# A recurrence and a mixture of experts on one core: the downs six units behind the ups, the gate products three, and a rebuilt head

## The reference, cut to what matters

```
xw = x @ Wx + b
h_t = tanh(xw_t + h_{t-1} @ Wh)                 # 32 steps, one after another
xn  = h * rsqrt(mean(h*h) + 1e-5) * norm_scale
vals, idx = top_k(xn @ wg + bg, 4); gates = softmax(vals)      # 4 of 16 experts
for each expert e:
    u = xn @ w1[e] + b1[e];  a = min(u[0::2], 7);  b = clip(u[1::2], -7, 7)
    y_e = (a * sigmoid(1.702 a) * (b + 1)) @ w2[e] + b2[e]
out = x + h + sum over e of gate_e * y_e
```

## Time and profile before

| | us |
|---|---|
| median of 3 runs | 108.16 (108.02 to 108.65) |
| profiled execution, its own time | 107.47 |
| its span, first to last instruction | 105.7 |
| TensorE busy | 98.3 (93%) |
| VectorE, GpSimd, ScalarE busy | 67.2, 64.7, 61.7 |
| chain that ended last, TensorE's share | 82% |

### The profile page before, as it was taken

The page is one execution under the profiler, slowest core; times in us unless marked ns, Lnnn a source line. Parts: engine busy times, 40 slices in busy tenths (PEclk is TensorE's granted clock), DMA queues, the critical chain, the costliest instruction groups (busy, mean ns, idle before and its releaser), DMA issues.

```text
span 105.7 us, 1704 instructions
## 1 busy us (share of the span) xinstructions
PE 98.3 (93%) x549; PEld 83.6 (79%) x549; DVE 67.2 (64%) x179; ACT 61.7 (58%) x143; POOL 64.7 (61%) x77
## 2 busy tenths in 40 slices
PE   7778899989999999999999979999999999999980
PEld 2557789978999999999999958888777777777660
DVE  0302357976827996589787997668566556666740
ACT  3354836999755586667736646666555666655400
POOL 6004447997890995639963799689544566544400
PEclk9999999999999999999999999999999999999999
DMA  2999920007930000895048911995100000000003
GB/s 66 224 378 338 374 92 0 0 9 254 398 147 3 0 6 6 212 372 212 5 141 228 366 67 20 274 364 207 34 6 0 3 0 0 0 0 0 0 0 99
DMA packets 5000, 12.97 MB, mean 123 GB/s; under 512 B 752, under 2 KB 1792, under 8 KB 4992
## 3 DMA queue, kind: packets, MB, share of 16 engines
q1 hardware_dynamic: 4672, 12.69, 35.5%
q10 hardware_dynamic: 320, 0.18, 0.6%
HBM read 12.28 MB, written 0.59 MB: 122 GB/s over the span
## 4 chain that ended last, share of the span: by engine, by line
PE 82%; ACT 7%; DMA 2%; DVE 2%; POOL 2%; issue 2%; POOLq 0%; DVEq 0%; ACTq 0%
PE psA L806 20%; PE psB L806 19%; PE psY L836 12%; PE psR L836 7%; PE psR L753 5%; PE psY L753 3%; PE psM L836 3%; PE psR L848 2%; DMA wx_x_sb<-in_wx_x 2%; PE psR L745 2%; PE psM L760 2%; ACT small_h L450 2%; ACT psA L494 2%; PE psM L767 1%; ACT psA L503 1%
## 5 line engine op out<-in xcount | busy, mean ns | idle before, releaser
L414 POOL TENSOR_TENSOR actg<-act,gate_cols 128x512 f32<-128x512 f32 x31 | 39.4, 1281 | 12.5 <-DVE act L713 10.7
L696 DVE TENSOR_SCALAR lin<-psB,one_b1b 128x256 f32<-128x256 f32 (+1 forms) x48 | 26.0, 568 | 18.8 <-PE psB L806 18.8
L494 ACT ACTIVATE psA<-psA,lim_b1a 128x256 f32<-128x256 f32 (+1 forms) x48 | 23.8, 513 | 23.2 <-PE psA L806 23.1
L713 DVE SCALAR_TENSOR_TENSOR act<-lin,psA 128x512 f32<-128x512 f32 x32 | 22.0, 686 | 1.8 <-ACT psA L503 0.6
L503 ACT ACTIVATE psA<-psA,limit_col 128x512 f32<-128x512 f32 x32 | 21.1, 659 | 0.8
L806 PE MATMUL psA<-xn_hi,w_hi 128*128 128x256 f32 (+1 forms) x48 | 18.9, 394 | 0.2
L836 PE MATMUL psY<-actg,w_sb 128*128 128x256 f32 x64 | 17.2, 391 | 0.8 <-POOL actg L414 0.8
L806 PE MATMUL psB<-xn_hi,w_hi 128*128 128x256 f32 (+1 forms) x48 | 16.0, 333 | 0.0
L806 PE MATMUL psB<-xn_lo,w_hi 128*128 128x256 f32 (+1 forms) x48 | 15.6, 324 | 0.0
L806 PE MATMUL psB<-xn_hi,w_lo 128*128 128x256 f32 (+1 forms) x48 | 15.5, 323 | 0.0
L806 PE MATMUL psA<-xn_hi,w_lo 128*128 128x256 f32 (+1 forms) x48 | 15.5, 323 | 0.0
(11 more groups left out here) (87 smaller groups left out, 133.7 us busy)
## 6 DMA issues: line engine op xcount, KB each, us to landing
gate_cols<-gate_rows SPq DMA_DIRECT2D x16, 512.0 KB, 5.7
w_sb<-in_w SPq DMA_DIRECT2D x4, 512.0 KB, 7.3
w_sb<-in_w SPq DMA_DIRECT2D x4, 256.0 KB, 8.3
wx_x_sb<-in_wx_x SPq DMA_DIRECT2D x1, 320.0 KB, 5.9
wx_x_sb<-in_wx_x SPq DMA_DIRECT2D x2, 128.0 KB, 2.7
out<-yT SPq DMA_DIRECT2D x2, 128.0 KB, 4.3
out<-yT SPq DMA_DIRECT2D x1, 192.0 KB, 1.9
small_h<-in_small ACTq DMA_DIRECT2D x1, 105.0 KB, 2.8
```

The source lines that it names most:

```text
L414: nc.gpsimd.tensor_tensor(by_pair(actg[:, u % SUM_DEPTH, w]), by_pair(act[:, u % ACT_DEPTH, w]), gate_block(u, w), ALU.mult).then_inc(actg ...
L494: last = nc.scalar.activation(psA[u % 2][:, o], psA[u % 2][:, o], ACT.Relu, scale=-1.0, bias=lim_b1a[:, e0 + k:e0 + k + 1])
L696: last = nc.vector.tensor_scalar(lin[:, v % 2, o], psB[v % 2][:, o], one_b1b[:, e0 + k:e0 + k + 1], LIMIT + 1.0, ALU.add, ALU.min)
L713: nc.vector.scalar_tensor_tensor(act[:, v % ACT_DEPTH, 0:w], lin[:, v % 2, 0:w], 1.0 - LIMIT, psA[v % 2][:, 0:w], ALU.max, ALU.mult).then_ ...
```

## The change

LAG goes from 4 to 6, POOL_LAG from 2 to 3, and the rings to 8 and 6 units. All w1_high copies that were in slots 0 to 2 move in front of slot 0. The x products get other places: psX holds that of tile 1, psY those of tiles 0, 3 and 4, psR those of 2, 5, 6 and 7. Tiles 1 and 2 are multiplied after steps 1 and 2, tile 3 after step 4, tile 4 after step 6, tile 5 after step 7, tile 6 behind the laying of rstd, and tile 7 alone in front of step 28 (slot 10). The sums of tile 1 go to psX with semaphores of their own (sum1_mm, mean_ready) and leave the turns of psM; the raw logits of tiles 0 and 1 are made together behind them. In slots below LAG the gates' transposes stand between the halves of the up, and their copies in front of the gelu. The scaling of the gates is one tensor_scalar per tile instead of one tensor_tensor per pair. GpSimd's powers stay in front of the gate product of their slot.

```diff
--- before.py
+++ after.py
@@ -42,15 +42,15 @@
     UNIT0 = [sum(E // r for r in EXPERTS[:c]) for c in range(NC + 1)]
     NU = UNIT0[NC]
     WARM, WARM_START = 512, 5
-    LAG = 4
-    POOL_LAG = 2
-    ACT_DEPTH, SUM_DEPTH = 6, 5
+    LAG = 6
+    POOL_LAG = 3
+    ACT_DEPTH, SUM_DEPTH = 8, 6
 
 
     GROUP0 = list(range(CHUNKS[0])) + list(range(CHUNKS[0], NT + 1, 2))
-    W1_AHEAD, W1_SHARED = 5, 3
-    XW_AT = [0, 0, 1, 1, 2, 1, 2, 3]
-    XW_LATE = 5
+    W1_SHARED = 3
+    XW_AT = [0, 3, 0, 1, 2, 1, 2, 3]
+    XW_LATE = 7
     NQ = NT // 2
     PW = 2 * P
 
@@ -160,12 +160,14 @@
         w1_half_ready = sem("w1_half_ready")
         w1_hi_ready = sem("w1_hi_ready")
         m_mm = sem("m_mm")
+        sum1_mm = sem("sum1_mm")
         raw_mm = sem("raw_mm")
         raw_read = sem("raw_read")
         m_read = sem("m_read")
         step_mm = sem("step_mm")
         step_done = sem("step_done")
         sq_ready = sem("sq_ready")
+        mean_ready = sem("mean_ready")
         xh_ready = sem("xh_ready")
         rstd_ready = sem("rstd_ready")
         xn_hi_ready = sem("xn_hi_ready")
@@ -276,7 +278,7 @@
         def xw_cols(j, n):
 
             k = XW_AT[j]
-            return (psY if j in (0, 2) else psR)[:, k * P:(k + n) * P]
+            return (psX if j == 1 else psY if j in (0, 3, 4) else psR)[:, k * P:(k + n) * P]
 
         def step_psum(t):
 
@@ -288,7 +290,7 @@
 
         def psM_turn(what):
 
-            order = [(k, g) for g in range(last_group(0) + 1) for k in ("stats", "rstd")]
+            order = [("stats", 0), ("rstd", 0), ("rstd", 1)]
             later = []
             for q in range(1, NQ):
                 g = pair_group(q)
@@ -364,7 +366,10 @@
             def power_rstd(g):
 
                 ts = group_tiles(g)
-                pool.wait_ge(m_read, psM_turn(("stats", g)))
+                if g == 1:
+                    pool.wait_ge(mean_ready, 1)
+                else:
+                    pool.wait_ge(m_read, psM_turn(("stats", g)))
                 nc.gpsimd.tensor_tensor(rstd[:, ts.start:ts.stop], meansq[:, ts.start:ts.stop],
                                         neg_half[:, :].to_broadcast([P, len(ts)]), ALU.pow).then_inc(rstd_ready, 1)
 
@@ -478,7 +483,7 @@
                 elif W1_AT <= t:
                     w1_high(t - W1_AT - (t > TL))
             acte.wait_ge(consts_ready, 1)
-            for k in range(HEAD - W1_AT - 2, 2 * W1_AHEAD):
+            for k in range(HEAD - W1_AT - 2, 2 * NP):
                 w1_high(k)
             for u in range(NU):
                 c, e0, r = unit(u)
@@ -498,19 +503,20 @@
                     for t in steps_at(u, 0):
                         tanh(t)
 
+                if u < LAG:
+                    for q in at(GATES_T, u):
+                        copy_gates(q)
                 acte.wait_ge(relu_done, u + 1)
                 w = width(u)
                 nc.scalar.activation(psA[u % 2][:, 0:w], psA[u % 2][:, 0:w], ACT.Gelu_apprx_sigmoid, scale=-1.0,
                                      bias=limit_col[:, :]).then_inc(swish_done, 1)
                 for t in steps_at(u, 1):
                     tanh(t)
-                for q in at(GATES_T, u):
-                    copy_gates(q)
+                if u >= LAG:
+                    for q in at(GATES_T, u):
+                        copy_gates(q)
                 for q in at(STATS, u + 1):
                     square(pair_group(q))
-                if u + W1_AHEAD < NP:
-                    w1_high(2 * (u + W1_AHEAD))
-                    w1_high(2 * (u + W1_AHEAD) + 1)
             acte.wait_ge(yT_ready, NC + 1)
             store(acte, slice((NT - 1) * P, NT * P), slice(P // 2, P))
 
@@ -528,11 +534,14 @@
 
                 ts = group_tiles(g)
                 n = len(ts)
-                dve.wait_ge(m_mm, psM_turn(("stats", g)))
-                mean = nc.vector.tensor_scalar(meansq[:, ts.start:ts.stop], psM[:, 0:n], 1.0 / H, EPS, ALU.mult,
-                                               ALU.add)
+                if g == 1:
+                    dve.wait_ge(sum1_mm, 1)
+                else:
+                    dve.wait_ge(m_mm, psM_turn(("stats", g)))
+                mean = nc.vector.tensor_scalar(meansq[:, ts.start:ts.stop], (psX if g == 1 else psM)[:, 0:n], 1.0 / H, EPS,
+                                               ALU.mult, ALU.add)
                 if g < CHUNKS[0]:
-                    mean.then_inc(m_read, 1)
+                    mean.then_inc(mean_ready if g else m_read, 1)
                 else:
                     copy_raw(ts, psM).then_inc(m_read, 1)
 
@@ -616,12 +625,12 @@
 
             def gates_scale(q):
                 settled()
-                ts = slice(2 * q, 2 * q + 2)
-                nc.vector.tensor_tensor(
-                    gates_w[:, ts, :].rearrange("p j (a b e) -> p j a b e", a=3, b=2)[:, :, :, 0, :],
-                    gate_sum[:, ts, :].rearrange("p j (a e) -> p j a e", a=1).to_broadcast([P, 2, 3, E]),
-                    inv[:, ts].rearrange("p (j a e) -> p j a e", a=1, e=1).to_broadcast([P, 2, 3, E]),
-                    ALU.mult).then_inc(scale_done, 1)
+                for j in pair_tiles(q):
+                    last = nc.vector.tensor_scalar(
+                        gates_w[:, j, :].rearrange("p (a b e) -> p a b e", a=3, b=2)[:, :, 0, :],
+                        gate_sum[:, j, :].rearrange("p (a e) -> p a e", a=1).to_broadcast([P, 3, E]),
+                        inv[:, j:j + 1], None, ALU.mult)
+                last.then_inc(scale_done, 1)
 
             def gates_low(q):
 
@@ -749,15 +758,17 @@
                 if t:
                     pe.wait_ge(step_done, t)
                 if t == TL * XW_LATE:
-                    x_wx(XW_LATE, NT - XW_LATE)
+                    x_wx(XW_LATE, NT - XW_LATE, start=False)
                 nc.tensor.matmul(step_psum(t), wh_sb, hT[:, t * N:(t + 1) * N], start=False, stop=True,
                                  skip_group_check=True).then_inc(step_mm, 1)
 
             def sums(g):
                 pe.wait_ge(sq_ready, g + 1)
-                turn(("stats", g))
+                if g != 1:
+                    turn(("stats", g))
+                bank = psX if g == 1 else psM
                 for k, j in enumerate(group_tiles(g)):
-                    last = nc.tensor.matmul(psM[:, k:k + 1], sq[:, j * P:(j + 1) * P], ones[:, :], start=True, stop=True)
+                    last = nc.tensor.matmul(bank[:, k:k + 1], sq[:, j * P:(j + 1) * P], ones[:, :], start=True, stop=True)
                 return last
 
             def raw_logits(ts, bank):
@@ -855,23 +866,23 @@
             pe.wait_ge(small_loaded, 16)
             for t in range(HEAD):
                 step(t)
-                if t == 3:
-                    x_wx(1, 1)
+                if t in (1, 2):
+                    x_wx(t, 1)
+                elif t == TL:
+                    x_wx(3, 1)
                 elif t == TL + 1:
                     pe.wait_ge(consts_ready, 1)
                     sums(0).then_inc(m_mm, 1)
                 elif t == TL + 2:
-                    pe.wait_ge(wg_ready, 1)
-                    raw_logits(range(0, 1), psB[0])
+                    x_wx(4, 1, start=False)
                 elif t == HEAD - 1:
                     lay_rstd(0)
-                    x_wx(2, 1)
-            sums(1).then_inc(m_mm, 1)
-            raw_logits(range(1, 2), psB[0]).then_inc(raw_mm, 1)
-            pe.wait_ge(step_done, HEAD)
-            x_wx(3, 1)
+            x_wx(5, 1, start=False)
+            sums(1).then_inc(sum1_mm, 1)
+            pe.wait_ge(wg_ready, 1)
+            raw_logits(range(0, 2), psB[0]).then_inc(raw_mm, 1)
             lay_rstd(1)
-            x_wx(4, 1, start=False)
+            x_wx(6, 1, start=False)
             for v in range(NU):
                 c, e0, r = unit(v)
                 if c == 0:
@@ -884,6 +895,8 @@
                 if v < LAG:
                     for t in steps_at(v, 0):
                         step(t)
+                    for q in at(GATES_T, v):
+                        transpose_gates(q)
                 if v >= 2:
                     pe.wait_ge(lin_done, v - 1)
                 if v == 0:
@@ -894,9 +907,6 @@
                 if v >= LAG:
                     for t in steps_at(v, 0):
                         step(t)
-                if v < LAG:
-                    for q in at(GATES_T, v):
-                        transpose_gates(q)
                 for q in at(STATS, v):
                     sums(pair_group(q))
                     raw_logits(pair_tiles(q), psM).then_inc(m_mm, 1)
```

## The result

| | before | after |
|---|---|---|
| median of 4 runs each, side by side | 108.35 (108.02 to 108.65) | 109.58 (109.45 to 109.62) |
| profiled execution, its own time | 107.47 | 109.45 |
| its span | 105.7 | 107.7 |

The account below looks back on a forecast made before the run. TensorE, busy 93% of the span, was taken as the bound. Terms -1.29, +0.22, +0.1, +0.36 and -0.16 gave -0.8, rounded to -0.9: span 104.8, median 107.3 us from 108.16, range 105.9 to 108.6.

Parts of the forecast that it names:

- Gate scaling: Two tensor_scalars instead of one tensor_tensor on VectorE: between -0.1 and +0.1 us, since VectorE has room.
- Slots 0 to 8: ScalarE alone paces slots 0 to 5, without downs; slot 8 starts at 35.65, -1.29 us not counting two deferred downs.
- rival 1: Slots 1 to 5 keep their pace near 2.4 us: +1.75, so +0.85 in all, 109.0; chance 0.14.
- rival 3: TensorE's fast clock level comes a slot later: +1.2, so +0.3 in all, 108.5; chance 0.08.
- Behind slot 8: From slot 8 on: two downs moved to the end at 0.87 each, +0.22 in slot 10, +0.36 net of two waits.
- LAG 6 at chunk 1: Slot 14: unit 8's down newly waits 1.3 us for VectorE's addition of chunk 0's residual; bounds 0.9 and 1.8.
- POOL_LAG 3: Slot 15: the wait before unit 11's down, held by a GpSimd product, goes; worth 0.94 us.
- Rival 4: The new wait in slot 14 isn't there, as the addition comes early enough: -2.2, 106.0; chance 0.10.
- Head: Before the first up: tile 1's sums no longer wait for xn, so the first up comes 0.34 us earlier.
- x products: Tiles 5 and 6 go from slot 6 to the head, -0.43 us; tile 7 costs 0.22 in slot 10.
- All w_hi copies before unit 0: Six more copies, 1.93 us, hide in ScalarE's 2.74 us idle time before unit 0's relu, freeing slots 0 to 2.
- The base: Differences were set against the profiled execution, span 105.7, time 107.47; the same sum was taken from the median, 108.16.

Follow-up runs that it names:

- e1: Changed kernel with the gates scaled by one tensor_tensor per pair again, as before the change; median 107.56 us, ratio 0.9909 to the kernel before.
- e3: Changed kernel with the two scalings per pair made as scalar_tensor_tensors instead of tensor_scalars; median 109.68 us, ratio 1.0109 to the kernel before.
- e4: e1 with the addition of a chunk's residual one slot earlier, behind act; median 107.36 us, ratio 0.9883 to the kernel before.
- e2: Kernel before with only the gate scaling changed, to two tensor_scalars per pair; median 108.88 us, ratio 0.9986 to the kernel before.
- e9: Kernel before with only LAG 6, POOL_LAG 3 and the deeper rings; median 108.10 us, ratio 1.0004 to the kernel before.
- e8: Kernel before with only the w_hi copies all moved in front of slot 0; median 109.62 us, ratio 1.0186 to the kernel before.
- e11: e7 with matmuls of constants filling idle TensorE in the head; median 106.81 us, ratio 0.9886 to the kernel before.
- e7: e4 with the gates scaled on ScalarE instead of VectorE; median 107.29 us, ratio 0.9937 to the kernel before.

## Why the prediction was wrong, by its own steps

By spans, the forecast was 104.8. Undoing one line gives 105.9, and the changed kernel has 107.7. So 1.8 us of the miss are the scaling, and 1.1 something else.

*Gate scaling, "somewhere between -0.1 and +0.1, and VectorE has room".* This is the step that failed: +2.0 by the medians (109.58 against e1's 107.56). I priced the instructions by their size and VectorE by its busy share. Both were beside the point. The duration is the wait for GpSimd's running subtraction or product, paid once an instruction (0.34 to 1.30 us here), and the instruction stands between `inv` and both `act` and the gates' transposes, which release TensorE in slots 2, 8 and 16. The trace of before held the hint: the same scaling takes 257 ns at least and 407 at the median for one size.

*Slots 0 to 8.* Forecast: slot 8 at 35.65, 3.23 earlier than before (1.29 and the two deferred downs of 0.95). In e1 it is at 36.87, so 1.2 of the 1.29 did not come. Chain of e1, slots 1 to 5:

```profile
18.38 1.35 PE psA L817 x6
...
22.47 0.80 PE psB L817 x6
23.27 0.14 PE psY L762 x2
23.41 0.79 PE psA L817 x6
24.20 0.30 PE psY L762 x2
24.49 0.80 PE psB L817 x6
...
30.17 0.89 DVE lin L705 x2
31.05 0.38 issue
31.43 0.69 DVE act L722
```

Three terms were mis-sized. A slot without a down is TensorE's and not ScalarE's: 0.80 + 0.14 + 0.79 + 0.30 = 2.03, not the 1.4 + 0.28 that I set against ScalarE's 1.92. That is rival 1's kind of loss, with another cause. And the fast level of the clock, 2.4 GHz by its passes of 0.12, begins at 19.4 in e1, where the six passes at 18.38 take 1.35, and not at 18.4: ScalarE gets unit 1's half at 19.75, not 19.1. That is the place of rival 3. The two make 0.65 + 3 x 0.11 = 1.0; slot 4 starts at 25.50, 0.9 late. The third is the pause before act of unit 5: the forecast let act follow the gelu and took 0.1 of the 0.51 to come back, but in e1 it is 0.51 again (the gelu ends at 30.92, act starts at 31.43), and act of unit 5 is 1.25 late, all that slot 8 is. What holds it is open: the gelu and lin (31.05) had both ended.

The fast level begins at 17.3 in the changed kernel, at 18.6 in e3, at 18.8 in e4, and in e2 only after 20.1. The Trainium skill's page on the clock ("TensorE: Matmul & The Clock Gate", Part 1) says that the moment varies from run to run. These traces are in line with that, but they are single executions of different kernels, whose first up starts between 14.68 and 15.22.

*Behind slot 8.* e1 takes 69.0 us from slot 8 to the end and before 66.8, 2.2 more; the forecast was two downs of 0.87, 0.22 and 0.36, or 2.3. Right. In it *LAG 6 at chunk 1*: a wait of 1.13 in both kernels where 1.3 was forecast, by the releaser that was named; and *POOL_LAG 3*: no wait before the down of unit 11. Rival 4 falls.

*Head*: -0.43 where -0.34 was forecast. Of the eight profiled kernels with this head seven start the first up between 14.68 and 14.96, and e4 at 15.22; the four with the head before at 15.03 to 15.27. *x products*: 0.22 in slot 10 as forecast, and steps 5 and 6 don't wait for the x load. *All w_hi copies before unit 0*: hidden, but with 0.59 to spare, so little.

*The base.* The sum was made from the profiled execution of before, 107.47. Its fellows lie higher: 108.35 in the median of 4, 108.52 to 109.16 in three rounds of 23. So e1's ratio, 0.9909, is as large as the forecast gain of 0.9 us, and yet does not bear the forecast out: its profiled run, 107.73, is 0.26 above that of before. In e1's round its lowest run, 107.16, is 0.5 below the lowest of before, and its highest, 108.39, is 5.2 below the highest. Kernels with LAG 6 keep close together (after 109.45 to 109.62, e9 107.65 to 109.45), those with LAG 4 spread (before 107.11 to 113.52 in one round, e2 108.29 to 112.00).

One long execution was profiled, e2's of 111.73, and its chain names the first gate columns on their way through DRAM:

```profile
22.33 2.99 DMA gate_rows<-gT
...
30.67 1.96 PE psY L836 x4
```

The write took 2.99 us there and 1.44 in e8, the product of unit 0 started at 29.35 (27.04 in before), TensorE waited 1.4 us for it before the down in slot 4, and the granted clock was 0.85 from 28 to 32 us and 0.72 from 32 to 36. In e9 the columns were late as well, product of unit 0 at 28.88, and TensorE, with this down two slots later, didn't wait for it. That this is what spreads the other runs with LAG 4 is likely from these two traces and not shown.

## What to carry to other kernels

- Where GpSimd streams tensors, count the VectorE instructions beside it that read only SBUF, not their elements: each can last until GpSimd's present subtraction or product is done (beside its powers they did not wait). Do the small ones in one instruction or on ScalarE, when the path to TensorE leads through them.
- Before one of two parallel chains is shortened, look how far the second is behind it; here neither the lags nor the early copies alone gained anything (ratios 1.0004 and 1.0186).
- Set a forecast against the spread of the runs, not against one profiled execution.

## What the runs showed of the hardware

- A VectorE scaling on SBUF operands ended some 0.05 us after the GpSimd subtraction or product it ran beside (0.12 with 96 elements, e1), and GpSimd's next began before VectorE's next: two scalings of 48 elements took 1.82 us in slot 14 where one of 96 took 0.67 (e1). The reciprocal (0.17) and the sums beside the same w_lo pieces did not wait, nor did `hot` (0.29) and w_lo on VectorE (0.42) beside a power of 1.33.
- TensorE's fast level began between 17.3 and 19.4 us in four kernels whose head is the same (after, e3, e4, e1). An early start of it (by 4.9 us in e11) was gone in the stretch after a gap of 0.95 us.
- The granted clock reads 1.00 in the first slow stretch of e7, with passes of 0.21 between starts, and 0.55 and 0.50 in e11, where the engine had been fast before. In a first slow stretch the spacing of passes tells the level, not the record.
